# Vision layer with routed experts: four groups' variances on GpSimd, filler products and the experts' table moved, a second buffer for the last pairs

## What is computed

```
h = patches(x) @ W                              # 64 images, 36 tokens each, 768 -> 192
h = h + attention(layernorm(h))                 # 12 heads of 16, causal, biases, 36 keys
p = softmax(layernorm(h) @ router_w.T)          # 8 experts; the two largest, renormalised
h = h + sum over the two of w_e * (gelu(n @ w1[e] + b1[e]) @ w2[e] + b2[e]),  n = layernorm(h)
```

## Time and profile before

| | |
|---|---|
| median of 3 runs (lowest, highest) | 413.14 us (410.65, 414.38) |
| profiled execution: its time, its span | 408.58 us, 406.8 us |
| busy: PE, PEld, DVE, ACT, POOL | 367.6, 327.6, 255.3, 218.6, 167.7 us |
| mean granted clock | 0.964 |

### The profile page before, as it was taken

One profiled execution on the slowest core, in us unless ns is written; L12 is line 12 of the kernel. 1 busy time (PEld: TensorE's weight loads), 2 busy tenths in 40 slices (PEclk: granted clock), 3 DMA queues, 4 the chain that ended last, 5 costly groups with the idle time before them and its releaser, 6 DMA issues.

```text
span 406.8 us, 14803 instructions
## 1 busy us (share of the span) xinstructions
PE 367.6 (90%) x5699; PEld 327.6 (81%) x5699; DVE 255.3 (63%) x687; ACT 218.6 (54%) x442; POOL 167.7 (41%) x203
## 2 busy tenths in 40 slices
PE   3989999989999999899897999999999999999910
PEld 3989989979889999885453689999999999999800
DVE  3696477787877867788686254555545554455426
ACT  5667687768777687662344244444444444444400
POOL 8116333345375532422100555555555555553310
PEclk9999999999999899999896999999999999999975
DMA  8974024432334223443060213222223222122058
GB/s 264 314 247 156 15 56 133 135 95 75 118 111 119 84 59 111 117 132 86 27 171 12 60 31 90 61 81 61 80 60 90 81 60 81 60 55 47 31 205 337
DMA packets 29705, 42.81 MB, mean 105 GB/s; under 512 B 12416, under 2 KB 19440, under 8 KB 29640
## 3 DMA queue, kind: packets, MB, share of 16 engines
q1 hardware_dynamic: 25512, 33.37, 27.1%
q0 software_dynamic: 4128, 8.50, 7.4%
HBM read 30.23 MB, written 9.67 MB: 98 GB/s over the span
## 4 chain that ended last, share of the span: by engine, by line
PE 75%; DVE 14%; DMA 3%; ACT 3%; issue 2%; POOL 2%; SPq 0%; POOLq 0%; DVEq 0%; ACTq 0%
PE PSA L1415 19%; PE PSA L1430 15%; PE PSA L1169 6%; PE PSA L1111 6%; PE PSA L1143 5%; PE PSA L1195 4%; PE PSA L1264 4%; PE PSA L1219 3%; PE PSA L1155 2%; PE PSA L1434 2%; PE PSA L1180 2%; PE PSA L1382 2%; DMA W2l<-yrows 2%; DVE H L1098 1%; PE PSA L1164 1%
## 5 line engine op out<-in xcount | busy, mean ns | idle before, releaser
L1415 PE MATMUL PSA<-YT,W1h 128*128 128x128 f16 x774 | 78.0, 219 | 1.5 <-DVE YT L1060 1.5
L1415 PE MATMUL PSA<-YT,W1l 128*128 128x128 f16 (+1 forms) x516 | 75.3, 220 | 0.0
L1430 PE MATMUL PSA<-W2h,PTR 128*128 x516 | 70.9, 246 | 0.3 <-DVE PTR L744 0.3
L543 POOL DMA_INDIRECT yrows<-KBR x43 | 43.1, 1001 | 63.4 <-DVE KBR L1075 63.4
L1415 PEld LDWEIGHTS PSA<-YT,W1h 128*128 x774 | 63.7, 98 | 5.6 <-DVE YT L1060 1.8
L1430 PE MATMUL PSA<-W2l,PTR 128*128 x258 | 63.5, 246 | 0.0
L730 ACT ACTIVATE PTR<-PSA 128x768 f32<-128x768 f32 x43 | 34.9, 812 | 51.1 <-PE PSA L1415 51.1
L538 POOL DMA_INDIRECT REG<-xrows,KBR x43 | 42.4, 987 | 43.6 <-DVE KBR L1050 27.4
L735 ACT ACTIVATE PTR<-PTR 128x768 f16<-128x768 f32 x43 | 36.3, 845 | 44.3 <-PE PSA L1434 44.2
L744 DVE SCALAR_TENSOR_TENSOR PTR<-PTR 128x768 f16<-128x768 f32 x43 | 41.2, 958 | 24.8 <-ACT PTR L735 24.8
L1075 DVE TENSOR_SCALAR KBR<-PSA,KBR 128x192 f32<-128x192 f32 x43 | 17.9, 417 | 52.9 <-PE PSA L1434 52.9
(11 more groups left out here) (179 smaller groups left out, 798.5 us busy)
## 6 DMA issues: line engine op xcount, KB each, us to landing
WSTG<-w SPq DMA_DIRECT2D x16, 384.0 KB, 3.9
WSTG<-w SPq DMA_DIRECT2D x16, 336.0 KB, 3.3
REG<-xt SPq DMA_DIRECT2D x12, 324.0 KB, 4.6
W1l<-xt SPq DMA_DIRECT2D x10, 324.0 KB, 6.8
VB<-VP SPq DMA_DIRECT2D x99, 19.1 KB
H<-hrows SPq DMA_DIRECT2D x6, 288.0 KB, 2.8
xrows<-REG SPq DMA_DIRECT2D x2, 800.2 KB
hrows<-H SPq DMA_DIRECT2D x1, 1296.0 KB
```

The costliest lines, as they stand in the source:

```text
L543: gp.indirect_dma_start(out=yrows, out_offset=bass.IndirectOffsetOnAxis(ap=TARGET[:, s:s + 1], axis=0), in_=YO[s % 2], in_offset=None).the ...
L1415: ins = nc.tensor.matmul(bank(2 * u + f // (FC // 2), 128, FC // 2 * ST_)[:, w:w + ST_], weights[a, c], YT[0:rows, at:at + ST_], start=k = ...
L1430: nc.tensor.matmul(bank(4 + u, ST_, C), GP[a][:, at:at + ST_], weights[b], start=(f, a, b) == (0, 0, 0), stop=False)
```

## The change

- Four groups (`ON_GPSIMD`, those in steps 5, 9, 13 and 17) have their variances and the refinement done by GpSimd: 12 small instructions, eight ahead of ScalarE's logarithm and four behind its exponential, between `norm1_row` and `norm2_row` of the step. The logarithm waits for the seventh of them. VectorE's ten instructions of these groups are gone.
- The second of the last pairs gets a buffer of its own in `KBR`; the copy of the third no longer waits for the router product of the second.
- The experts' table (three VectorE instructions) is made behind the one-hot matrices; its readers wait on a new semaphore `chosen`.
- `at_low` of parts 1 and 2 is one instruction of 13 tiles where there were 14 of one tile; the third part has 18 tiles instead of 16.
- Unread products: 4 to 6, 1 to 3, 22 to 18, then (4, 4, 4) to (4, 10, 0) ahead of the parts, and 24 to 14 ahead of the first gathered rows; 11, 1 and 28 stay.

```diff
-        PARTS = [(0, 14), (14, 28), (28, TOPK * NT)]
+        PARTS = [(0, 13), (13, 26), (26, TOPK * NT)]
+        ON_GPSIMD = range(2, group(PAIRED))
+        PSTEPS = 12
+        def pair_xt(t):
+            return KBR[:, 0:3 * TT].bitcast(F16) if t == PAIRS[1][0] else XT[:, :]
@@ gpsimd
+            def group_variances(n):
+                a, b = NORMS[n]
+                base = PSTEPS * (n - ON_GPSIMD.start)
+                gp.wait_ge(st2_done, b - NT)
+                s = ST[:, a * 6:b * 6].rearrange("p (t c) -> p t c", c=6)
+                mean, dm, var = MEAN[:, a:b], DM[:, a:b], VAR[:, a:b]
+                nc.gpsimd.tensor_tensor(mean, s[:, :, 1], s[:, :, 4], ALU.add).then_inc(group_done, 1)
+                nc.gpsimd.tensor_tensor(dm, s[:, :, 1], s[:, :, 4], ALU.subtract).then_inc(group_done, 1)
+                nc.gpsimd.tensor_tensor(var, s[:, :, 2], s[:, :, 5], ALU.add).then_inc(group_done, 1)
+                gp.wait_ge(group_done, base + 2)
+                nc.gpsimd.tensor_tensor(dm, dm, dm, ALU.mult).then_inc(group_done, 1)
...
@@ gpsimd, the loop over steps
+                if group_end(i - 2) and group(i - 2) in ON_GPSIMD:
+                    group_variances(group(i - 2))
+                    group_refine(group(i - 2))
                 for t in norm2_at(i):
                     norm2_row(t)
@@ scalar, inverse_deviation
-                act.wait_ge(mv_done, 9 * n + 7)
+                if n in ON_GPSIMD:
+                    act.wait_ge(group_done, PSTEPS * (n - ON_GPSIMD.start) + 7)
+                else:
+                    act.wait_ge(mv_done, 9 * on_vector(n) + 7)
@@ scalar, pair_out
                 act.wait_ge(n2_mm, t + 2)
-                act.wait_ge(r_mm, t)
+                if t == PAIRS[1][0]:
+                    act.wait_ge(s_mm, NT)
+                else:
+                    act.wait_ge(r_mm, PAIRED if t == PAIRED else t - 2)
@@ vector, step
-                    if group_end(i - 2):
+                    if group_end(i - 2) and group(i - 2) not in ON_GPSIMD:
                         variances(group(i - 2))
...
@@ vector, the one-hot matrices
                 if p < 2:
-                    for n in range(a, b):
-                        nc.vector.tensor_scalar(AT_LOW[:, n * ST_:(n + 1) * ST_], IOTA, LOW[:, n:n + 1], None, ALU.is_equal).then_inc(low_placed, 1)
+                    nc.vector.tensor_tensor(at_low(a, b), IOTA.unsqueeze(1).to_broadcast([TT, b - a, ST_]),
+                                            LOW[:, a:b].unsqueeze(2).to_broadcast([TT, b - a, ST_]), ALU.is_equal).then_inc(low_placed, 1)
@@ tensor
-            unread(4)
+            unread(6)
             pair_router(PAIRS[0][0])
             pair_transpose(PAIRS[1][0])
             unread(1)
             pair_transpose(PAIRS[2][0])
             pair_router(PAIRS[1][0])
-            unread(1)
+            unread(3)
             pair_router(PAIRS[2][0])
-            unread(22)
+            unread(18)
...
             for p, (a, b) in enumerate(PARTS):
-                unread(4)
+                unread((4, 10, 0)[p])
...
-            pe.wait_ge(count, 10)
+            pe.wait_ge(chosen, 3)
...
             load_experts(0, AHEAD)
-            unread(24)
+            unread(14)
```

More of the change, by code:

```diff
@@ L345, in build, with on_vector @@
         NORMS += [(NT + t, NT + min(t + GROUP, NT)) for t in range(0, NT, GROUP)]
+        ON_GPSIMD = range(2, group(PAIRED))
+        PSTEPS = 12
+        def on_vector(n):
+            return n - len(ON_GPSIMD) if n >= ON_GPSIMD.stop else n
         def up_biases(p):
@@ L489, in norm1_low @@
                 nc.gpsimd.tensor_tensor(xp[:, C:2 * C], two(XF[0], t, C), xp[:, 0:C], ALU.subtract).then_inc(n1_lo, 1)
+            def group_variances(n):
[9 more added lines that the diff above has]
+                nc.gpsimd.tensor_tensor(dm, dm, dm, ALU.mult).then_inc(group_done, 1)
+                gp.wait_ge(group_done, base + 4)
+                nc.gpsimd.tensor_scalar(dm, dm, 0.25 * C, None, ALU.mult).then_inc(group_done, 1)
+                nc.gpsimd.tensor_scalar(mean, mean, 0.5, None, ALU.mult).then_inc(group_done, 1)
+                gp.wait_ge(group_done, base + 5)
+                nc.gpsimd.tensor_tensor(var, var, dm, ALU.add).then_inc(group_done, 1)
+                gp.wait_ge(group_done, base + 7)
+                nc.gpsimd.tensor_scalar(HV[:, a:b], var, -0.5 / (C * S_X ** 2), -0.5 * EPS / S_X ** 2, ALU.mult, ALU.add).then_inc(group_done, 1)
@@ new lines, in group_refine @@
+            def group_refine(n):
+                a, b = NORMS[n]
+                base = PSTEPS * (n - ON_GPSIMD.start)
+                rs, t1 = RS[:, a:b], DM[:, a:b]
+                gp.wait_ge(ln_done, 2 * n + 2)
+                gp.wait_ge(group_done, base + 8)
+                nc.gpsimd.tensor_tensor(t1, rs, HV[:, a:b], ALU.mult).then_inc(group_done, 1)
+                gp.wait_ge(group_done, base + 9)
+                nc.gpsimd.tensor_tensor(t1, t1, rs, ALU.mult).then_inc(group_done, 1)
+                gp.wait_ge(group_done, base + 10)
+                nc.gpsimd.tensor_scalar(t1, t1, 1.5, None, ALU.add).then_inc(group_done, 1)
+                gp.wait_ge(group_done, base + 11)
+                nc.gpsimd.tensor_tensor(rs, t1, rs, ALU.mult).then_inc(group_done, 1)
@@ L491, in norm2_row @@
             def norm2_row(t):
-                need(gp, rs_done, group(t) + 1)
+                if group(t) in ON_GPSIMD:
+                    gp.wait_ge(group_done, PSTEPS * (group(t) - ON_GPSIMD.start + 1))
+                else:
+                    need(gp, rs_done, on_vector(group(t)) + 1)
                 need(gp, n2_lo, 2 * t - 2)
@@ L693, in pair_out @@
                 act.wait_ge(n2_mm, t + 2)
-                act.wait_ge(r_mm, t)
-                nc.scalar.activation(XT[:, :], bank(pair_bank(t), 128, 6 * TT, F16), ACT.Copy).then_inc(n2_done, 2)
+                if t == PAIRS[1][0]:
+                    act.wait_ge(s_mm, NT)
+                else:
+                    act.wait_ge(r_mm, PAIRED if t == PAIRED else t - 2)
+                nc.scalar.activation(pair_xt(t), bank(pair_bank(t), 128, 6 * TT, F16), ACT.Copy).then_inc(n2_done, 2)
             for i in range(NT - 1):
@@ L839, in late_rows @@
             def late_rows(t):
-                dve.wait_ge(rs_done, group(t) + 1)
+                dve.wait_ge(rs_done, on_vector(group(t)) + 1)
                 if t == PAIRS[1][0]:
@@ L1244, in pair_router @@
                         ins = nc.tensor.matmul(bank(router_bank(t), TT, 512)[:, ROUT + m * E:ROUT + (m + 1) * E],
-                                               two(XT, t + m, 3 * TT)[:, n * TT:(n + 1) * TT],
+                                               pair_xt(t)[:, (3 * m + n) * TT:(3 * m + n + 1) * TT],
                                                WR[a][:, c * E:(c + 1) * E], start=k == 0, stop=k == len(ROUTER_PRODUCTS) - 1)
```

48 lines of the change are left out of this document (26 added, 22 removed).

## The result

| | before | after |
|---|---|---|
| median (lowest, highest), us | 411.97 (410.65, 414.38) | 417.47 (416.21, 418.58) |
| ratio, 95% interval | | 1.0126 [1.0063, 1.0188] |
| profiled execution: time, span, us | 408.58, 406.8 | 418.58, 416.7 |
| busy: PE, DVE, POOL, us | 367.6, 255.3, 167.7 | 372.4, 250.0, 182.8 |
| mean granted clock | 0.964 | 0.953 |

The medians are of four runs each, the runs of before shown earlier among them. The forecast was 408.7 us with a range of 400.5 to 414. The result lies outside, on the other side of before. The two profiled executions differ by more than the medians, 9.9 us in the span: that of before is a quick one, and that of after is the slowest of its four.

The account below looks back on a forecast made before the run. It took TensorE's chain to bound the kernel, with stalls around four groups and waits behind the loop. +2.0 (pipeline) - 6.4 (behind the loop) = -4.4 us gave 408.7 us as median, range 400.5 to 414.

Parts of the forecast that it names:

- What bounds the kernel: Steps around a group: 1.45 us over two ordinary ones, TensorE waiting for VectorE's `y_lo` and for GpSimd; five places behind the loop.
- Part A, the stall: Group steps: weight pieces block GpSimd's variances, the logarithm starts 1.95 us later, TensorE waits 1.9 us ahead of `project`.
- Part A, the sum: Four group steps: waits of 1.9 to 2.0 replace 1.45 us, +0.5 a group, +2.0 us in all.
- rival C: Steps behind the groups: each `project` wait brings the clock to 0.50 for 3 us; 416.7 to 419.7 us; chance 0.06.
- Rival A: Group steps: GpSimd's four-column instructions slip between VectorE's, blocking does not bite; -12.2, 400.9 us; chance 0.18.
- Part B: Behind the loop: five terms for routing, table, one-hot matrices and first expert, -6.4 us, ends -7 and -2.7.
- (1) to (4): Behind the loop: own buffer -0.3, earlier ranks -1.0, later experts' table -1.1, one-hot matrices -2.8; table read 5.2 us sooner.
- rival B: Behind the loop: clock falls at TensorE's new idle places, before the ranks or over the register load; 412.4 us; chance 0.14.
- (4): One-hot matrices: one 13-tile instruction takes 1.8 us instead of 2.37 for 14 small ones; table read another 2.8 us sooner.
- (5): From table read to first expert: about 5.2 us instead of 6.4 with 14 unread products for 24, -1.2 us.
- From span to median: Whole kernel: 404.2 us for an execution like the profiled one, plus 4.6 to the median, gives 408.7 us.
- In the experts "nothing moves": Expert tiles behind the first expert's start: no change in time.

Follow-up runs that it names:

- e9: Kernel with only the edits behind the loop (VectorE variances), one weight piece's low half in odd steps, two in even: 404.40 us, 0.9830 of before.
- e4: Changed kernel with eight unread products in each of the four waits ahead of `project`: 408.52 us, 0.9872 of before.
- e8: e2 with the unread products counted as before the change: 408.23 us, 0.9929 of before.
- e11: e2 with the experts' table made ahead of the slots again: 408.31 us, 0.9935 of before.
- e2: Changed kernel with all variances back on VectorE, so only the edits behind the loop: 408.50 us, 0.9878 of before.
- e1: Kernel before with only the four groups' variances moved to GpSimd: 421.72 us, 1.0196 of before.
- e12: e9 with 23 unread products instead of 18 ahead of the ranks: 402.26 us, 0.9824 of before.
- e3: Changed kernel (GpSimd variances) with VectorE's two weight pieces of the group steps moved behind `probs_lo` and `logits`: 406.99 us, 0.9857 of before.
- e10: Changed kernel (GpSimd variances) with one weight piece's low half in odd steps, two in even: 412.81 us, 1.0020 of before.
- e7: e2 with eight unread products ahead of the third expert tile's `up`: 408.43 us, 0.9923 of before.

## Why the prediction was wrong, step by step

**What bounds the kernel.** Right: the wait for `y_lo`, and VectorE's work ahead of it. e9 gains by shortening just that.

**Part A, the stall.** Right in its length and its links. 0.20 us an instruction was forecast and measured, the logarithm 3.3 us behind the statistics (some 3.4 forecast), a wait of 1.9 us ahead of `project` (1.8 to 2.1 measured), none ahead of `norm2_transpose`, GpSimd's instructions beside the pieces at 0.9 to 1.0 us in steps 5 and 9, and one of 1.8 in steps 13 and 17. The Trainium skill, SBUF — State Buffer, section "Who interferes with whom", says that of a VectorE instruction with two SBUF inputs and a GpSimd one that reads SBUF the later one blocks. The traces of steps 5 and 9 agree: 0.98 us against 0.20. In steps 13 and 17 the one held for 1.78 us had, by its timeline, started 0.10 us ahead of the piece.

**Part A, the sum: here it failed.** "So 1.9 to 2.0 replace 1.45 us: +0.5 a group, +2.0 us for four" takes a wait of TensorE at its own length. The long steps grew by 2.0, 2.2, 2.9 and 2.2 us, 9.3 in all. The stall itself is near the forecast: 0.5 us a group was put down, and 0.7 is measured at full clock (e4 against e8 and e11: 2.7 us for four). The step that failed is the term for the clock, which the sum put at nothing: at 0.50 behind each wait it took 7.3 us, 1.8 a group. The mechanism stood in the text, as rival C, with its place and a price of 1.5 us a group; it had a chance of 0.06, and it was bound to the upper end of the stall, so that it needed +4 besides. The argument against it, that waits of 0.65 and 0.57 go by today at a mean clock of 0.964, says nothing on a wait three times as long. The trace of before had such a wait: the 1.79 us ahead of part 1. Behind it TensorE was busy for 5.62 of 6 us at a granted clock of 0.50:

```profile
217.00:223.00 6.00, 5.62 (x53) 2.78 (x48) 2.98 (x15) 0.95 (x1) 0.00 (x0) 0.50 0.01 3
```

Rival C's 416.7 to 419.7 holds the result, in part by luck: its stall of +4 was 2.7, its 6 us of clock were 7.3, and part B gave less than its -6.4.

**Rival A** is refuted: the pieces block GpSimd in all four groups of the change, two instructions of 0.91 to 0.98 us in steps 5 and 9, one of 1.78 and 1.79 in steps 13 and 17.

**Part B.** Forecast -6.4, and -4.0 in the profile after. (1) to (4) were forecast at -5.2 for the read of the table: e2 gives 5.2, the change itself 4.0, with 1.4 lost to the clock in the 32 products, which is rival B in another place than I put it. The 5.2 also hold what before lost to its own clock from 217 to 223. (4) has a small slip in its column rate: 946 columns at 1.05 ns and 0.07 us are 1.06 us, not 1.10; the wide instruction took 1.88 us where 1.8 was put down. (5) failed: "First expert at about 5.2 behind the read", -1.2, is 2.6 to the second gather, some 2 for its rows and 0.6 for what is behind. In the change the second gather is issued 2.60 us behind the read, its rows are used 2.67 us after that, and the transpose and VectorE's copy take from 235.43 to 236.51, 1.08: together 6.35, and it was 6.38 before. Ten products more or less are 0.1 us (6.49 in e8 with 24, 6.38 in e2 with 14).

**From span to median.** I subtracted from the profiled execution and added 4.6 us. In medians the halves are +8.8 (e1) and -4.4 (e2), together +4.4, and +5.5 was measured.

**In the experts "nothing moves".** Wrong by 1.5 us: the third tile started 6.58 us behind the first (5.04 before), and so much of part B's gain is lost again. The products of the first tile's `up` took 2.7 instead of 1.9 us, since the clock fell in them, and ScalarE's first GELU then began 0.7 us behind the last of them, where it had been at once before. In e2 it was 6.58 too, with the clock up until just ahead of the third tile; there the first GELU began 3.46 us behind the first product of the `up` it needs, where it was 1.91 before, 3.44 in e11, 2.83 in e8 and 1.90 in e12. No run tells why.

## What to carry to other kernels

Price a wait of TensorE at its length plus what the clock may take behind it: here the 2 us waits ahead of `project` cost some 1.8 us more each, and unread products in the same place gave it back. Look in the trace at hand for a wait of that length and at the clock behind it. Before small work goes to GpSimd, look at what VectorE runs in that stretch with two inputs in SBUF; and before it goes anywhere, ask whether the late result is late because of it or because of longer work that has slack, here the weight pieces, one of which was shifted by a step: the four long steps took 27.3 us in e9 against 30.3 in e11, 3.0 less, with no work moved to another engine. The medians, on one chip, are 404.4 against 408.3; e11 also has its table ahead of the slots, which is 1.07 us in the traces.

## What the runs showed of the hardware

- A GpSimd instruction of 4 columns that started 0.01 to 0.06 us behind VectorE's piece was held in every case read: 0.97 and 0.98 us in the change, 1.01 in e3, 0.96 and 1.02 in e10. One that started ahead was not always free: 0.10 us ahead it took 0.21 and 0.20 us in steps 5 and 9 of the change, 0.10 and 0.11 us ahead 1.78 and 1.79 in steps 13 and 17; 0.13 us ahead it took 0.20 in e3 and 1.04 in e10. The pieces of steps 5 and 9 are W1's and the others W2's, which no run takes apart.
- Between the two pieces of steps 5 and 9 VectorE lets one GpSimd instruction in (0.98 and then 0.91 us). Between those of steps 13 and 17 it doesn't: one is held for 1.78 us, through both pieces. So one or two of the twelve are hit, and the delay is about the same.
- The same wait doesn't always bring the clock down: 0.98 us ahead of `project` did in e7 (a granted clock of 0.79 and 0.64 in the two windows of 3 us behind it) and did not in e8 (1.00), 0.61 us did in e3. All four waits of 1.8 to 2.1 us ahead of `project` did, in the change and in e1, and so did the 1.79 us of before. But TensorE waited 1.87 us in e8 and 1.93 in e10 ahead of the third expert tile, and the clock stayed at 1.00. What decides is not shown.
- Behind the loop the fall came in another place whenever one was taken away (e7, e8), but these are single executions, and falls behind short waits differ from one to the next: the loop is the same code in e2, e7, e8 and e11, and the clock fell in its second and third long steps in e2, in the first and fourth in e7, and in none in e8 and e11. So that a prevented fall moves on is not shown. Only e12, with no wait ahead of `project` in its long steps and 0.27 us ahead of the ranks, had no fall from 85 to 300 us.
